# Cross attention of a two-layer decoder: scores computed a second time in place of turned probabilities, and context keys of three chunks made within their own batch

## The reference, cut to what matters

```
q, k, v   = x Wq, x Wk, x Wv      (q and k rotated)
ck, cv    = ctx Wk, ctx Wv        (375 context rows)
own       = softmax(q k^T / 4 + mask) v
context   = softmax(q ck^T / 4) cv * tanh(gate)
x         = x + (own + context) Wo
```

## Time and profile before

| | |
|---|---|
| median of 3 runs | 1869.06 us |
| the profiled execution | 1871.72 us |
| its span in the trace | 1869.9 us |
| PE busy | 1792.0 us (96% of the span) |
| DVE busy | 998.8 us (53%) |
| ACT busy | 606.0 us (32%) |
| POOL busy | 409.6 us (22%) |
| granted TensorE clock, mean | 0.984 |

### The profile page before, as it was taken

How to read it: one execution, slowest core, us unless ns; L and a number is a source line. 1 busy time by engine, 2 the same in 40 slices (tenths; PEclk the granted TensorE clock), 3 DMA queues, 4 the chain that set the end, 5 groups by cost and what they waited for, 6 DMA issues and landing times.

```text
span 1869.9 us, 29060 instructions
## 1 busy us (share of the span) xinstructions
PE 1792.0 (96%) x11730; PEld 1179.7 (63%) x11730; DVE 998.8 (53%) x1892; ACT 606.0 (32%) x1931; POOL 409.6 (22%) x488
## 2 busy tenths in 40 slices
PE   7999999999999999999889999998999999999998
PEld 6766666646665665666555888876577674444444
DVE  4765666426666666557644111116645455565887
ACT  1233222315555565555640111110312213232511
POOL 2432323512020220120003000006121020002476
PEclk9999999999999999999998999999999999999999
DMA  9100002000000000000214988965000021643011
GB/s 377 42 1 1 1 1 107 1 15 18 18 18 15 4 18 18 1 17 2 113 69 174 368 331 327 339 254 198 27 1 1 1 107 50 250 161 124 3 38 40
DMA packets 31109, 170.62 MB, mean 91 GB/s; under 512 B 3865, under 2 KB 3865, under 8 KB 17185
## 3 DMA queue, kind: packets, MB, share of 16 engines
q1 hardware_dynamic: 28416, 161.43, 22.9%
q0 software_dynamic: 2560, 7.34, 1.3%
HBM read 155.91 MB, written 16.52 MB: 92 GB/s over the span
## 4 chain that ended last, share of the span: by engine, by line
PE 83%; DVE 9%; POOL 4%; ACT 2%; issue 2%; DMA 1%; SPq 0%; POOLq 0%; DVEq 0%
PE PS L1142 8%; PE PS L985 6%; PE PS L1222 6%; PE PS L936 6%; PE PS L1019 5%; PE PS L1058 4%; PE PS L1010 4%; PE PS L1286 4%; PE PS L1182 4%; PE PS L1151 4%; PE PS L1255 3%; PE PS L1042 3%; PE PS L1273 3%; PE PS L1078 2%; PE PS L993 2%
## 5 line engine op out<-in xcount | busy, mean ns | idle before, releaser
L2046 POOL TENSOR_TENSOR rstd<-veps,mhalf 112x1 f32<-112x1 f32 (+1 forms) x76 | 58.0, 764 | 577.2 <-DVE veps L1315 554.0
L1142 PEld LDWEIGHTS PS<-R,W 128*128 128x128 f32 x1344 | 155.8, 195 | 11.8 <-issue 11.8
L1142 PE MATMUL PS<-R,W 128*128 128x128 f32 x1344 | 156.2, 278 | 2.2 <-DVE R L1610 2.2
L1439 DVE TENSOR_REDUCE nmx<-PS 112x2 f32<-112x750 f32 x128 | 114.0, 931 | 81.4 <-PE PS L1042 81.4
L1910 ACT ACTIVATE R<-PS,nmx 112x375 f32<-112x375 f32 x256 | 142.9, 573 | 3.7 <-DVE nmx L1439 3.7
L936 PE MATMUL PS<-xT,W 128*128 128x224 f32 x640 | 127.1, 359 | 1.1 <-DMA W<-in_w0kv 0.8
L936 PEld LDWEIGHTS PS<-xT,W 128*128 128x128 f32 x640 | 123.0, 194 | 7.7 <-issue 5.5
L1617 DVE TENSOR_TENSOR R<-R,PS 128x512 f32<-128x512 f32 x21 | 14.5, 688 | 201.7 <-PE PS L1142 201.7
L1387 DVE TENSOR_TENSOR x<-x,PS 112x512 f32<-112x512 f32 x40 | 27.5, 687 | 170.0 <-PE PS L985 82.4
L1255 PE MATMUL PS<-W 128*128 128x512 f32 x256 | 117.6, 602 | 0.0
L985 PE MATMUL PS<-W,R 128*112 128x512 f32 x256 | 113.7, 597 | 0.0
(11 more groups left out here) (291 smaller groups left out, 3233.7 us busy)
## 6 DMA issues: line engine op xcount, KB each, us to landing
W<-in_we SPq DMA_DIRECT2D x63, 1024.0 KB, 8.3
W<-in_entwT SPq DMA_DIRECT2D x8, 1024.0 KB, 7.3
W<-in_entpw SPq DMA_DIRECT2D x8, 1024.0 KB, 8.5
W<-in_ctxT SPq DMA_DIRECT2D x8, 750.0 KB, 4.2
R<-in_ctxT SPq DMA_DIRECT2D x8, 750.0 KB, 8.4
R<-in_ctx SPq DMA_DIRECT2D x8, 750.0 KB
xs_rows<-in_x SPq DMA_DIRECT2D x3, 1792.0 KB, 38.2
R<-xs_rows SPq DMA_DIRECT2D x21, 256.0 KB, 9.1
```

The lines of the kernel that those rows point to most:

```text
L1142: o = e.matmul(PS[:, m, c * 128:(c + 1) * 128], gate_up(j % 3, k, off + c * 128), BT[:, j % 2, k, :], start=k == 0, stop=k == 3)
L1439: e.tensor_reduce(nmx[0:S, par, r:r + 2], PS[0:S, r:r + 2, 0:SC], AX.X, ALU.max, negate=True).then_inc(*up("cmax", (b, c, par, r)))
```

## The change

- `xs` and `xc` become one step for each parity: 64 tasks in place of 96. `slot` writes out the order within a task, with three places for fill steps, and `cross` deals the fill out to them by SHARE.
- The context probabilities are no longer turned. The scores are computed a second time the other way round (`xst`): 12 matmuls with 32x125 keys stationary and the 112 columns of q moving, into the banks of the first scores. The row maximum must then be known per column. It goes in through the product: each parity's keys get a row of ones (`ones_at`) in the zero columns of q, and the negated maxima (NM), turned by one transpose (`xq`), are added into that row of QM by DVE (`qa`). ACT exponentiates 1344 columns in one instruction (`ce`).
- The sums come from columns of ones in the values (`one_at`). Each result tile OU then has the sum in one row of each 32. For a chunk DVE spreads these rows by two stream shuffles (128x224 each) and takes the reciprocal of all of it (128 x 448), and POOL multiplies by the gain, by OU and adds, in four instructions (`xd`). The steps `xr` and `xb` go.
- `ck`, `cv`, `vx` and `xw` are split into halves of 4 matmul instructions. The keys of chunks 1 to 3 are made at the head of the fill of their own batch; only chunk 0's are made in the batch before. The load of CT then waits for the last `ck` also.
- tanh(gate) comes as a column; the `ck` copies out of PSUM are two each (one for each parity); the scratch memory of software DMAs is set to 4096.

```diff
+SHARE = (0.3, 0.25, 0.45)
+def slot(n, fill):
+    out = []
+    here, behind, last = [TASKS[m] if 0 <= m < len(TASKS) else None for m in (n, n - 1, n - 2)]
+    if here:
+        out += [("xc", *here), ("cm", *here, 0), ("cm", *here, 2)]
+    if last:
+        out += [("xv", *last), ("xcv", *last), ("xu", *last)]
+        if last[2]:
+            out.append(("xd", *last[:2]))
+    out += fill[0]
+    if behind:
+        out.append(("xt", *behind))
+    if here:
+        out += [("xq", *here), ("xm", *here, 0), ("qa", *here)]
+    out += fill[1]
+    if here:
+        out += [("xst", *here), ("ce", *here), ("xm", *here, 1), ("xm", *here, 2), ("xe", *here)]
+    return out + fill[2]
...
+        keys = context(b)[2:8] if b else []
+        fill = [("load", "ct", b + 1)] * (0 < b < NBATCH - 1)
+        then = context(b + 1)[:2] + context(b + 1)[8:] + values_x(b + 1) if b + 1 < NBATCH else [("load", "front", j) for j in (1, 2, 0)]
...
+        fill = keys + fill + then
         late = expert_rows(range(6)) if b == NBATCH - 1 else []
+        fixed = {(3, 2): [("xw", b - 1, 0)], (4, 0): [("xw", b - 1, 1), ("stats", 2, b - 1)]} if b else {}
+        unit = sum(cost(s) for s in fill + late) + sum(cost(s) for some in fixed.values() for s in some)
+        unit, due = unit / 8, 0.0
+        for i in range(8):
+            if i == 2:
                 fill += late
+            windows = []
+            for k in range(3):
+                some = fixed.get((i, k), [])
+                due += 1.7 * SHARE[k] if b == NBATCH - 1 else unit * SHARE[k] - sum(cost(s) for s in some)
+                while fill and (due > cost(fill[0]) / 2 or (i, k) == (7, 2)):
+                    due -= cost(fill[0])
+                    some.append(fill.pop(0))
+                windows.append(some)
+            out += slot(8 * b + i, windows)
...
     if k == "xc":
+        return (0, 1, 2, 3), 4, [[("cexp", a), ("masked", a)]] * 4
...
+                for r in range(4):
+                    ro = slice(32 * r, 32 * r + 32)
+                    o = e.matmul(PS[0:S, r, SC:SC + S], QM[z][ro, c, par, bcol(i)], KX[z][ro, c, bcol(i)], start=True,
+                                 stop=True)
+                o.then_inc(*up("scores", ("xs", b, c, par)))
...
+            def xq(b, c, par):
+                m = bank(("xq", b, c, par))
+                w.wait_ge(*at("cmax", (b, c, par, 2)))
+                t = e.transpose(PS[:, m, 0:S], NM[0:S, par, :], ident[0:S, 0:S])
+                t.then_inc(*up("p_turned", ("xq", b, c, par)))
+            def xst(b, c, par):
+                z, i = (b // UB) % 2, b % UB
+                w.wait_ge(*at("masked", (b, c, par)))
+                w.wait_ge(*at("qa", (b, c, par)))
+                for t_ in range(3):
+                    for r in range(4):
+                        ro = slice(32 * r, 32 * r + 32)
+                        o = e.matmul(PS[0:KC, r, bcol(t_)], KcT[b % 2][par][ro, c, t_ * KC:(t_ + 1) * KC],
+                                     QM[z][ro, c, par, bcol(i)], start=True, stop=True)
+                o.then_inc(*up("scores", ("xst", b, c, par)))
...
+            def qa(b, c, par):
+                q = QM[(b // UB) % 2][:, c, par, bcol(b % UB)]
+                w.wait_ge(*at("p_turned", ("xq", b, c, par)))
+                e.tensor_tensor(q, q, PS[:, bank_of["xq", b, c, par][0], 0:S], ALU.add).then_inc(*up("qa", (b, c, par)))
...
+            def xd(b, c):
+                z = c % 2
+                w.wait_ge(*at("ou", (b, c, 1)))
...
+                for par in range(2):
+                    e.stream_shuffle(SH[:, z, par], OU[:, z, par], [(16, 0)[par]] * 32).then_inc(*own())
+                settled()
+                e.reciprocal(SH[:, z], SH[:, z]).then_inc(*up("recip", (b, c)))
...
+            def ce(b, c, par):
+                w.wait_ge(*at("scores", ("xst", b, c, par)))
+                e.activation(PC[0:KC, par], PS[0:KC, 0:4, 0:3 * S], ACT.Exp).then_inc(*up("cexp", (b, c, par)))
...
+            def xd(b, c):
+                w.wait_ge(*at("recip", (b, c)))
...
+                e.tensor_tensor(t, t, gain[:, c].rearrange("p a k -> p (a k)").unsqueeze(2).to_broadcast([128, 4, S]),
+                                ALU.mult).then_inc(*up("g_own", ("xd", b, c, 0)))
+                sem = done(0)
+                e.tensor_tensor(SH[:, z], SH[:, z], OU[:, z], ALU.mult).then_inc(*sem)
+                sem = done(1)
+                e.tensor_tensor(SH[:, z, 0], SH[:, z, 0], SH[:, z, 1], ALU.add).then_inc(*sem)
+                w.wait_ge(*at("g_own", ("xd", b, c, 2)))
+                e.tensor_tensor(OXT[:, b % 2, c, :], SH[:, z, 0, 0], SH[:, z, 0, 1], ALU.add).then_inc(*up("oxt", (b, c)))
```

## The result

The changed kernel takes 2011.32 us, median of 4 runs (2009.25 to 2014.55), against 1868.62 for the kernel before: ratio 1.0764, 95% interval 1.0745 to 1.0783. The forecast was 1984 us. The profiled execution took 2012.6 us with a span of 2010.4, 140.5 more than before.

A forecast was written before the change was run, and what follows sets the result against it. PE was taken as the bound (83% of the span; busy 527.7 of the cross attention's 551.0 us). Profiled 1871.7 us plus 59 for the chain and 56 for the clock gave 1987, less 2.7 for the median: 1984 us, range 1922 to 2032.

The forecast's parts named there:

- The reciprocal: DVE's reciprocal of 448 columns in `xd`, ahead of mask and `qa` in parity 1 tasks: 2.86 us, 32 times.
- The estimate of 3.7 us: Reciprocal at eight cycles of 0.96 GHz an element: 28 us more over 32 of them; not used in the sum.
- The waits: In the cross attention, PE idles 2.4 to 2.6 us before `xst` in each of 32 parity 1 tasks.
- The task by task table: Batch 2's fill dealt over eight tasks: parity 0 lasts 32.9 us, parity 1 42.4, a batch 75.3.
- PE's saving: PE's work in the cross attention: 4.8 us less a batch, 39 us over eight, if PE stays the bound.
- The clock: Waits in 32 tasks halve PE's granted clock in three of four: 24 falls of 2.35 us, +56 us.
- Rival 1: Cross attention's chain without the clock: PE's waits do not bring it down, 1928 us; chance 0.18.
- Outside the stage: Stages other than the cross attention stay as before; smaller scratch, touching 32 indirect DMAs, costs 0 to 5 us.
- Rival 2: Reciprocal cheap at 0.62 us, PE stays the cross attention's bound: 11 us less, 1858; chance 0.07.
- Rival 3: Heavier still: `xst` nearer to `xb`'s price, or long clock falls each time: up to 1984 + 50; chance 0.12.
- keys are moved, not added: Key calls on PE, three of 2.7 us, leave batch 0's stretch and enter batch 7's; no instruction added.
- +59: Cross attention with each task a closed chain: 609 to 610 us against 551.0, at full clock.

The follow-up runs named there:

- e2: The changed kernel with `xd` (shuffles and reciprocal on DVE, products on POOL) moved behind `qa` in a task's order: 1927.08 us, ratio 1.0307.
- e5: The changed kernel with 150 matmuls whose result nobody reads put ahead of `xst` in 28 tasks: 1975.64 us, ratio 1.0564.
- e6: The kernel before with only the smaller scratch for software DMAs (4096): 1869.26 us, ratio 1.0002.
- e1: The changed kernel with a product of the same tile in the reciprocal's place, so without the division: 1915.58 us, ratio 1.0244.
- e4: The changed kernel with the keys of chunks 1 to 3 made in the batch before their own again: 2028.63 us, ratio 1.0853.
- e12: The changed kernel with sums of both parities merged and a halved reciprocal (128x224), left in the change's place: 2008.11 us, ratio 1.0753.

## Why the prediction came out near

Its sum stood at 1987 us for the profiled execution, which took 2012.6. The 26 us between are taken term by term here.

1. **The reciprocal** was put at 2.86 us from the line through the earlier trace rows. It takes 2.95, 94.5 us in all against 92. The estimate of 3.7 us that the prediction worked out from the Trainium skill ("VectorE: DVE Perf Modes", section "First, the fixed hardware budget") is not what the trace shows.
2. **The waits.** A stage of 609.5 us with 518.5 - 39 of PE's work has 130 us of waits in it; 137 were measured. Parity 1 waits 2.2 us in the mean (2.4 to 2.6 was said, in each task; 22 of the 32 have 1.9 or more), and e2 shows that `xd`'s place causes that. The task by task table was coarser than its sum: 44 of the 137 us are waits for other things than the anchors, several of which it has no term for: maxima behind a norm's statistics, turned norms, key chunks that need two evictions.
3. **PE's saving** was put at 39 us and is 29: 489.8 us of work at full clock against 518.5. `xst` is not to blame: its calls take 0.85 us from start to start, where 0.89 was said (the 0.92 of the timeline runs to the end of the last matmul). What the sum lacks is the last matmul in front of a wait, which no next one overlaps: a key instruction takes 0.48 us there and 0.32 from start to start elsewhere. Such ends make 15 us at 98 waits, against 5 at 25 before. That is the size of what is missing, but the fill steps grew by 16 us and the tasks' own steps shrank by 5 more than was said, which I can't give to single causes.
4. **The clock.** 24 falls were predicted and 24 found. They cost 56.6 us, and 56 stood in the sum. The size of the term is right, and e5 confirms that waits of PE bring it: 41 us of clock back with the waits filled. That the count is right to the unit is partly luck. The prediction had all 24 behind the waits of the 32 parity 1 tasks; 17 are there, and seven stand at other waits, for the maxima, a norm, a load of CT and the parity 0 anchors among them. Rival 1, the same chain without the clock (1928), is out.
5. **Outside the stage** nothing was charged; there it is 8.3 us: 4.8 ahead (the stage starts at 430.5 for 425.7) and 3.5 behind. e6 shows that the scratch parameter costs the kernel before nothing. Ahead of the stage PE's waits are 4.6 us longer, and most of it is one wait for a product of POOL in the self attention, 3.7 us before and 6.6 now. POOL's new setting of ones stands just ahead of that product, but takes only 0.15 us (376.77); what delays the rest is open. Behind the stage the time at 1.2 GHz goes from 26.9 to 33.0 us, half of which difference is 3 of the 3.5.

So 7 + 10 + 1 + 8 = 26. The reciprocal's 2.5 us more of DVE lie within the waits. Rival 2 was to gain 11 us with a product in the reciprocal's place and PE as the bound. e1 gives it that price and loses 2.4%: the premise was false on the chip, and even with it the claim is wrong, as 75 us of waits are left, 21.8 of them parity 0's for the anchors, which have nothing to do with the reciprocal. Rival 3 was heavier in `xst`, which fell with 0.85, and in long falls each time: 11 of the 24 are longer than 3.4 us, and their mean is 5.1, where 5.3 was said. The step "keys are moved, not added" was counted at nothing and was worth 17 us in the change's favour (e4), 9 of them clock and 6 waits.

What the prediction did not see is that most of its own +59 was not a price but an order: the first two instructions that PE needed could have gone ahead of the one that nobody was waiting for.

## What to carry to other kernels

For an engine that works in written order, price a long instruction by what stands behind it: ask for each one who waits for its result and who waits for its neighbours' results, and put those that nobody waits for last. Moving the reciprocal behind two instructions of 0.6 and 0.3 us gave 84 us of 143; making it almost free gave 96, and both together with better fill still didn't reach the kernel before: PE's work had become 26 us less, and its waits 38 us more. That the closed chain within a task makes these is argued, not shown. Where PE is left waiting for some 2 us again and again, add a second charge for the clock to the sum of waits, here 57 us on 137.

## What the runs showed of the hardware

**A reciprocal goes by the column.** 1, 8, 64, 224 and 448 columns take 0.164, 0.203, 0.541, 1.553 and 2.953 us: 5.6 to 6.3 ns for each further column, six times a product's 1.03.

**POOL's products stretch small instructions of DVE.** Beside e12's merge, `xm`'s maximum with a constant shows it, an instruction of 112x4 elements; by line in the changed kernel:

```profile
L1418 DVE TENSOR_SCALAR sx<-sx x64: 169/366/1036, 438.5 to 1087.9; 112x4 f32<-112x4 f32 x64
```

At 692.40 it takes 1.03 us while POOL's second product of `xd` (692.28, 1.13 us) runs; at 683.69, with POOL idle, 0.17. The other side pays too: POOL's product of 128x448 is 1.13 us there and 1.61 in e2 at 649.02, beside a DVE instruction with two inputs. The Trainium skill, "SBUF — State Buffer", section "Who interferes with whom", says that VectorE in a mode that uses both of its port pairs, which a `tensor_scalar` can enter, contends with GpSimd for the pair they share, and that the instruction that comes later is fully blocked. The trace agrees for the instruction of four columns, which ends with POOL's product at 693.4. It is 0.17 us in each of the 26 that have no POOL instruction beside them, and 0.22 to 1.04 in the 38 that have one. Moving work to POOL was counted as free in the prediction; the 64 of these take 35.1 us, where 64 at 0.17 would be 10.9.

**The length of a single wait does not decide whether the clock falls.** In the changed kernel's stage 13 stretches at 1.2 GHz are 3.4 us, 10 are 6.8 and one is 10.2. Of the 18 waits of PE of 2.4 us or more, 15 have a fall begin in them or within 2.2 us of their end, and three have none, one of 2.94 us (964.11) among them. In the kernel before all six of that length after the start were followed by a fall, which is what the prediction went by. Two falls (1058.42, 1078.90) have no wait longer than 1.42 us next to them.
